# Two graph-attention networks on one core: heads turned through a direct SBUF exchange, two jobs of VectorE given to ScalarE, mask work and turns in other places

## The chip, the cores and the metric

The kernel runs on one core of one Trainium2 chip. The metric is device time in microseconds (us) of a whole launch; the kernel before takes 2327.34 us, the median of 3 runs (2326.52 to 2328.55).

## What is computed

Sixteen graphs of 512 nodes with 256 features pass through two networks. All is float32.

```python
# first network, 3 layers (L0)
si = x @ attn_w[l, :d];  sj = x @ attn_w[l, d:]
scores = leaky_relu(si[:, :, None] + sj[:, None, :] + attn_b[l])        # slope 0.2
attn = softmax(where(adjacency + I > 0, scores, -inf))
h = layernorm(x + attn @ x, g1[l], beta1[l])
x = layernorm(h + gelu(h @ W1[l] + b1[l]) @ W2[l] + b2[l], g2[l], beta2[l])
# x = layernorm(input + x), then the second network, 8 heads of 32 (L1)
xh = heads(x @ W_proj);  a_src, a_dst = xh . W_att
att = softmax(where(A > 0, leaky_relu(a_src + a_dst + b_att), -1e30))
out = relu(att @ xh)
# result: layernorm(x + out)
```

## The kernel before

Nodes lie on the 128 partitions in four groups (T = 4). A unit is one layer of one graph: 48 units, and the loop `for g in range(REGULAR)` takes them in a fixed order. A **slot** g runs, on TensorE (PE), the feed-forward of unit g and the attention of unit g+1; beside them the heads of the second network are made for older graphs. From slot 8 on the slots come in threes, and g % 3 says what else is in them. I call them kinds 2, 0 and 1, in the order in which they follow each other. Per graph, heads 0, 1, 2 are made in kind 2, heads 3, 4 in kind 0, heads 5, 6, 7 in kind 1. `turned(g)` are the heads made in the slot before; they have to change rows with columns before PE can use them. Two ways are used:

- heads 0, 3 and 5 are turned by PE (`turn`, PSUM bank pT) and copied back by ScalarE (ACT) (`turned_out`);
- heads 1, 2, 4, 6 and 7 (`moved`) are turned in 32x32 blocks by VectorE (DVE), L903 in `turn_blocks`, and the blocks then change partitions by DMA from SyncE's queue (SP), `move`, L410: four transfers out to `blocks_dram` (L416), a wait for all four, one transfer back (L419). 66 heads go this way.

PE uses four heads at once (`attend_heads`, L1282) in kinds 2 (heads 0 to 3) and 0 (heads 4 to 7), `heads_back` (L1290) follows two products later. In kind 2 that is after the first-layer product f = 1, in kind 0 after f = 3 (`spent_behind`).

PE's order in a slot: eight products f = 0 to 7 of the first feed-forward matrix (L1330), among them the spreading of a row of targets over the partitions (`first_target_row`, L1219, "trow"); then 16 **pieces** of the second matrix (L1341), and among these pieces the turns and products of the first network's attention (`attention`, L1240 and L1258), then the transposes of the new state (L1317). Three counts set how many pieces stand ahead of, inside and behind the attention. Product f = 0 waits until DVE has emptied bank 0 of the slot before (`fed_forward(graph, 0)`, L959), product f = 3 until it has emptied bank 1.

DVE's order in a slot is long and serial: end of the layer of the slot before (L959, L778, L966, L972), scores (L837), the masked targets and their maxima (L846, L853), the first network's exponents (L867 adds the maximum), the next head's targets, turns, the four groups of the attention (L913, L915, L920) with a head between them, the sums of an ended graph, mask work (`find_lone`, `make_masks`, `keep_masks`), the last head. ACT does leaky relu (L529, L536), exponentials (L542 for heads, L547 for the first network, out of pT), gelu (L560), normalisation (L576) and copies. POOL raises the variance to the power -1/2 (L500) and makes the shift (L505).

Every engine keeps its own order, written out by hand, and waits on semaphores. The functions that the change touches:

## Time and profile before

| | |
|---|---|
| median of 3 runs | 2327.34 us |
| profiled execution, its own time | 2329.5 us |
| its span | 2327.7 us |
| PE busy | 2187.7 us (94%) |
| DVE busy | 1863.9 us (80%) |
| ACT busy | 1636.4 us (70%) |
| DMA queue of SP | 313.72 MB, 42.5% of 16 engines |
| chain that ended last | PE 71%, DVE 20%, ACT 5% |
| mean granted PE clock | 0.984 |

The span is the time between the first and the last instruction that the profiler recorded. Busy time is the sum of the instructions of an engine; matmuls are pipelined, so PE's busy share is not its share of peak. A row of a timeline is start, duration, engine, line, operation, tiles, count and, in brackets, the idle time before it and what ended it. Consecutive instructions overlap a little in the records, so the step from one start to the next is what an instruction costs.

### The profile page before, as it was taken

The numbers are of one execution on the slowest core, as the hardware profiler recorded it, in microseconds if no ns is written. First come the engines' busy times: TensorE is split into PE (matmuls) and PEld (weight loads), VectorE is DVE, ScalarE is ACT, GpSimd is POOL, SyncE is SP. The second block draws the span as 40 slices with busy tenths as digits, with TensorE's granted clock in tenths as the row PEclk, the third lists the DMA queues.
The fourth block names the chain that finished last, engine by engine and source line by source line (L and its number), as shares of the span: only waits on it lengthen the run. The fifth ranks groups of instructions, "written<-read, shape, count | busy, mean of one in ns | idle before, by whom it ended". The sixth has DMA issues, their size and how long they took to land.

```text
span 2327.7 us, 31621 instructions
## 1 busy us (share of the span) xinstructions
PE 2187.7 (94%) x10117; PEld 1525.1 (66%) x10117; DVE 1863.9 (80%) x5743; ACT 1636.4 (70%) x3151; POOL 201.8 (9%) x200
## 2 busy tenths in 40 slices
PE   5999998999999999999999999999999999999766
PEld 3766666676667667667766766676676667667453
DVE  5566587688888888888888888888888888877867
ACT  2344467777787777778777777777777777778676
POOL 0000100010101001010100101010010101001000
PEclk9999999999999999999999999999999999999888
DMA  6011133227455362735436274553627455364201
GB/s 219 1 36 55 47 108 127 86 87 236 131 179 157 114 213 86 245 122 186 150 123 206 85 241 125 178 158 114 212 86 229 138 171 165 97 202 153 92 28 37
DMA packets 162145, 315.74 MB, mean 136 GB/s; under 512 B 10392, under 2 KB 82620, under 8 KB 153532
## 3 DMA queue, kind: packets, MB, share of 16 engines
q1 hardware_dynamic: 161980, 313.72, 42.5%
q8 instruction: 82, 1.34, 0.2%
q14 instruction: 83, 0.68, 0.1%
HBM read 235.82 MB, written 77.86 MB: 135 GB/s over the span
## 4 chain that ended last, share of the span: by engine, by line
PE 71%; DVE 20%; ACT 5%; issue 2%; POOL 1%; DMA 1%; DVEq 0%; SPq 0%; POOLq 0%; ACTq 0%
PE ffn L1341 19%; PE av L1258 14%; PE av L1330 10%; PE ffn L1330 10%; PE pT L1240 7%; PE av L1282 4%; DVE prob L846 3%; DVE prob L837 2%; DVE stats L778 2%; PE av L1317 1%; DVE lone L806 1%; PE av L1365 1%; PE trow L1365 1%; DVE xs L972 1%; DVE xs L966 1%
## 5 line engine op out<-in xcount | busy, mean ns | idle before, releaser
L1341 PE MATMUL ffn<-w_sb,G 128*128 128x256 f32 x3072 | 724.1, 381 | 12.5 <-ACT G L560 12.5
L1341 PEld LDWEIGHTS ffn<-w_sb,G 128*128 128x128 f32 x3072 | 571.1, 191 | 94.1 <-ACT G L560 18.1
L846 DVE CUSTOM_DVE_ANT_0 prob<-trow,mask 128x512 f32<-128x512 f32 x676 | 438.5, 686 | 31.7 <-PE trow L1219 19.6
L1330 PE MATMUL ffn<-hT,w_sb 128*128 128x512 f32 x768 | 364.0, 601 | 4.4 <-DVE xs L959 1.3
L1330 PE MATMUL av<-hT,w_sb 128*128 128x512 f32 x768 | 358.2, 596 | 0.0
L500 POOL TENSOR_TENSOR rstd<-veps,mhalf 128x4 f32<-128x4 f32 x127 | 170.5, 1342 | 2087.4 <-DVE veps L774 2087.4
L536 ACT ACTIVATE prob<-prob,s 128x512 f32<-128x512 f32 x484 | 329.4, 715 | 7.7 <-DVE aw_row L853 4.3
L542 ACT ACTIVATE prob<-prob,nm 128x512 f32<-128x512 f32 x464 | 329.2, 714 | 0.0
L1240 PEld LDWEIGHTS pT<-ident,prob 128*128 128x128 f32 x1648 | 208.2, 144 | 134.0 <-issue 103.3
L1240 PE MATMUL pT<-ident,prob 128*128 128x128 f32 x1648 | 251.3, 278 | 27.2 <-DVE prob L908 14.6
L1330 PEld LDWEIGHTS ffn<-hT,w_sb 128*128 128x128 f32 x768 | 140.1, 191 | 152.2 <-issue 134.1
L1330 PEld LDWEIGHTS av<-hT,w_sb 128*128 128x128 f32 x768 | 139.0, 191 | 148.3 <-issue 148.3
L560 ACT ACTIVATE G<-av,cols 128x512 f32<-128x512 f32 x192 | 130.1, 685 | 148.2 <-PE av L1330 148.1
L1258 PE MATMUL av<-xs,prob 128*128 128x257 f32 x960 | 229.9, 381 | 0.3 <-ACT prob L547 0.3
L560 ACT ACTIVATE G<-ffn,cols 128x512 f32<-128x512 f32 x192 | 131.4, 684 | 87.1 <-PE ffn L1330 86.6
L1258 PEld LDWEIGHTS av<-xs,prob 128*128 128x128 f32 x960 | 175.7, 190 | 22.5 <-ACT prob L547 0.7
L576 ACT ACTIVATE xs<-prob,shift,rstd 128x256 f32<-128x256 f32 x180 | 93.4, 590 | 133.3 <-POOL shift L505 133.2
L529 ACT ACTIVATE prob<-prob,small 128x512 f32<-128x512 f32 x192 | 128.6, 723 | 73.0 <-DVE small L853 73.0
L903 DVE STREAM_TRANSPOSE blocks<-prob 128x2048 f32<-128x2048 f32 x66 | 152.4, 2309 | 16.4 <-DMA blocks_dram<-blocks 16.0
L867 DVE TENSOR_SCALAR prob<-prob,small 128x512 f32<-128x512 f32 x192 | 93.3, 486 | 83.7 <-ACT prob L529 72.7
L547 ACT ACTIVATE prob<-pT 128x512 f32<-128x512 f32 x192 | 113.3, 591 | 54.0 <-PE pT L1240 53.5
L913 DVE RECIPROCAL small<-av 128x1 f32<-128x1 f32 x192 | 31.2, 163 | 137.5 <-PE av L1258 136.0
(164 smaller groups left out, 2739.5 us busy)
## 6 DMA issues: line engine op xcount, KB each, us to landing
w_sb<-in_L_gnn_W SPq DMA_DIRECT2D x92, 1024.0 KB, 8.8
blocks_dram<-blocks SPq DMA_DIRECT2D x264, 256.0 KB, 4.2
prob<-blocks_dram SPq DMA_DIRECT2D x66, 1024.0 KB, 4.9
trow<-rows_dram SPq DMA_DIRECT2D x127, 256.0 KB, 3.7
adj_sb<-in_adj SPq DMA_DIRECT2D x16, 1024.0 KB, 9.0
xin<-in_x SPq DMA_DIRECT2D x16, 512.0 KB, 6.0
x0r<-in_x SPq DMA_DIRECT2D x16, 512.0 KB, 10.0
out<-o SPq DMA_DIRECT2D x15, 512.0 KB, 6.9
```

The source lines that it names most:

```text
L500: nc.gpsimd.tensor_tensor(rstd[which][:], veps[which][:], mhalf[:], ALU.pow).then_inc(s_rstd, 1)
L529: nc.scalar.activation(prob0[:, t, :], prob0[:, t, :], ACT.Prelu, bias=col0[:, t:t + 1], scale=1.0, alpha=SLOPE).then_inc(s_score0, 1)
L536: nc.scalar.activation(m, m, ACT.Prelu, bias=s1[q // HEADS % 2][:, t, q % HEADS:q % HEADS + 1], scale=1.0, alpha=SLOPE).then_inc(s_score1, 1)
L542: nc.scalar.activation(m, m, ACT.Exp, bias=largest(q)[:, t:t + 1], scale=1.0, accum_out=sums_of(q)[:, 0, t:t + 1]).then_inc(s_exp, 1)
L547: nc.scalar.activation(prob0[:, t, :], pT[t % BANKS][:], ACT.Exp).then_inc(s_prob, 1)
L560: nc.scalar.activation(G[:, f, :], ff1[f % len(ff1)][:], ACT.Gelu, bias=b1_col[:, l, f:f + 1]).then_inc(s_gelu, 1)
L846: return v.tensor_tensor_reduce(out=out_[:, t, :], in0=targets, in1=mask[:, t, :], scale=1.0, scalar=LEAST, op0=ALU.add, op1=ALU.max, accu ...
L903: v.transpose(blocks[:].rearrange("p b (x i) -> p x b i", i=BLOCK), ring(q)[:].rearrange("p t (j b i) -> p (t j) b i", b=BLOCKS, i=BLOCK)) ...
L1240: last = te.transpose(pT[bank][:, j * P:(j + 1) * P], src[:, t, j * P:(j + 1) * P], ident[:])
L1258: last = te.matmul(av0[t % BANKS][:, 0:D + 1], prob0[:, t, j * P:(j + 1) * P], state(graph, l)[:, j, :], start=j == 0, stop=j == T - 1)
L1330: last = te.matmul(ff1[f % len(ff1)][:], w1_sb[:, weights_of(g) % STAGES, dt, f * P:(f + 1) * P], hT[:, dt, :], start=dt == 0, stop=dt == ...
L1341: last = te.matmul(ffn[part][:, at:at + D], G[:, f, t * P:(t + 1) * P], w2_sb[:, weights_of(g) % STAGES, f, :], start=f == 0, stop=f == FT ...
```

## The change

Line numbers of the kernel before are used throughout.

- `move` no longer goes through DRAM. For each turned head it issues 16 transfers from SBUF to SBUF, 32 partitions by 512 numbers (64 KB) each, all counted on one semaphore. DVE's next turn and PE's `attend_heads` wait for all 16.
- The first network's exponent leaves DVE: L867 is gone, ACT takes the maximum as the bias of its exponential in place (192 more instructions), and PE's turned result is copied out by ACT instead of going through the exponential. The interleaving of these with the exponentials of a held head ends: they come first, the held head's behind them.
- The normalisation of an ended graph (`graph_out`, L1047) moves to ACT in the regular slots.
- Turns are placed elsewhere: kind 0 now turns heads 1 (ahead of the attention) and 2 (behind it), kind 1 head 4 (ahead), kind 2 heads 6 and 7 as before. Before, kind 1 turned 2 and 4.
- `make_masks` is cut in two: `mask_edges` stands ahead of the attention of kind 0, `mask_diagonal` where it was, and `find_lone` moves to the end of kind 2.
- `spent_behind` is 1 in every slot (the change's condition on head 5 is false), so kind 0 attends heads 4 to 7 after f = 1 and takes them back after f = 3.
- The counts of pieces: one more ahead of the attention, one fewer behind it.

```diff
 def turned_ahead(g):
-    return [q for q in turned(g) if moved(q)][:1] if g % 3 != 1 else []
+    return [q for q in turned(g) if moved(q)][:1] if g > min(FIRST_MADE) + 1 else []
 def turned_behind(g):
-    if g % 3 == 1:
-        return [q for q in turned(g - 1) + turned(g) if moved(q)][-2:] if g > 1 else []
-    return [q for q in turned(g) if moved(q)][1:] if g % 3 == 2 else []
+    return [q for q in turned(g) if moved(q)][len(turned_ahead(g)):]
 def spent_behind(g):
-    return 3 if g % 3 == 0 else 1
+    return 4 if g % 3 == 0 and HEADS - 3 in BY_BLOCKS else 1
+def masked(g):
+    return g // 3 + 1 if g > 3 and g % 3 == 0 and g // 3 + 1 < GRAPHS else None
...
             def move(q):
                 n = moves(q) - 1
-                i = n % BANKS
                 sp.wait_ge(s_block, n + 1)
-                if n >= BANKS:
-                    sp.wait_ge(s_moved, 16 * (n - BANKS + 1))
-                for a in range(BLOCKS):
-                    sp.dma_start(blocks_dram[i, :, :, a, :].rearrange("b j n -> j b n"),
-                                 blocks[a * BLOCK:(a + 1) * BLOCK, :, :]).then_inc(s_left, 16)
-                sp.wait_ge(s_left, 16 * BLOCKS * (n + 1))
-                sp.dma_start(ring(q)[:], blocks_dram[i].rearrange("b j a n -> (b j) a n")).then_inc(s_moved, 16)
+                for b in range(BLOCKS):
+                    for a in range(BLOCKS):
+                        sp.dma_start(ring(q)[b * BLOCK:(b + 1) * BLOCK, a, :],
+                                     blocks[a * BLOCK:(a + 1) * BLOCK, b, :]).then_inc(s_moved, 16)
...
+            def first_exponential(t):
+                act.wait_ge(s_score0, c("score0"))
+                nc.scalar.activation(prob0[:, t, :], prob0[:, t, :], ACT.Exp, bias=nm0[:, t:t + 1], scale=1.0).then_inc(s_arg, 1)
             def probabilities(t):
                 act.wait_ge(s_pt, c("pt"))
-                nc.scalar.activation(prob0[:, t, :], pT[t % BANKS][:], ACT.Exp).then_inc(s_prob, 1)
+                nc.scalar.copy(prob0[:, t, :], pT[t % BANKS][:]).then_inc(s_prob, 1)
+            def first_network_probabilities(u, scored):
+                first_exponential(0)
+                for t in range(1, T):
+                    if t >= scored:
+                        score0(u, t)
+                    first_exponential(t)
+                    probabilities(t - 1)
+                probabilities(T - 1)
...
+                if leaving(g) is not None:
+                    normalise(LAST, o1, o1, s_out)
...
                 for q in turned_ahead(g):
                     turn_blocks(q)
+                if masked(g) is not None:
+                    mask_edges(masked(g) % 2)
                 attention(graph2, l2, *new[1:2])
...
                 elif g > 3 and g % 3 == 2:
                     keep_masks(g // 3 % 2)
-                elif g > 3 and g % 3 == 0 and g // 3 + 1 < GRAPHS:
-                    find_lone((g // 3 + 1) % 2)
-                    make_masks((g // 3 + 1) % 2)
+                    if g // 3 + 2 < GRAPHS:
+                        find_lone(g // 3 % 2)
+                elif masked(g) is not None:
+                    mask_diagonal(masked(g) % 2)
...
-                ahead, inside, behind = (4, (1, 1), (1, 1, 1, 1)) if four is None else (2, (2, 1), (2, 1, 2, 1))
+                ahead, inside, behind = (5, (1, 1), (1, 1, 1, 0)) if four is None else (3, (2, 1), (2, 1, 1, 1))
```

Three places show the order before and now. First DVE at the end of a slot of kind 2, from the turn of head 7 (`prob_7`) to the emptying of bank 1 (second L959; in the change L974) and the statistics behind it. Before:

```order
L903 STREAM_TRANSPOSE blocks<-prob_7 128x16x4x32
L951 TENSOR_TENSOR xs<-xs,bias_row 128x4x256
L959 TENSOR_TENSOR xs<-ffn,xs 128x2x256
L816 COPY mask_0<-mask_0 128x2048
L819 SCALAR_TENSOR_TENSOR mask_0<-ident,own,mask_0 128x128 x4
L824 TENSOR_SCALAR mask_0<-mask_0,lone 128x512 x4
L846 ISA prob_2,small<-trow,mask_1 128x512
```

In the change:

```order
L918 STREAM_TRANSPOSE blocks<-prob_7 128x16x4x32
L966 TENSOR_TENSOR xs<-xs,bias_row 128x4x256
L974 TENSOR_TENSOR xs<-ffn,xs 128x2x256
L835 COPY mask_0<-mask_0 128x2048
L838 SCALAR_TENSOR_TENSOR mask_0<-ident,own,mask_0 128x128 x4
L843 TENSOR_SCALAR mask_0<-mask_0,lone 128x512 x4
L825 TENSOR_REDUCE lone<-adj_sb 128x4
L827 TENSOR_SCALAR lone<-lone 128x4
L829 TENSOR_SCALAR lone<-lone 128x4
L865 ISA prob_2,small<-trow,mask_1 128x512
```

Three instructions of `find_lone` are new here, ahead of head 2 (`prob_2`). Second, DVE in a slot of kind 0, from the maxima of head 4 to the emptying of bank 0. Before:

```order
L853 SCALAR_TENSOR_TENSOR nm<-small 128x4
L1039 SCALAR_TENSOR_TENSOR o<-o,l1x 128x1024
L778 BN_STATS stats<-o 128x6 x4
L769 BN_AGGR mv_out<-stats 128x2 x4
L774 TENSOR_SCALAR veps<-mv_out 128x4
L951 TENSOR_TENSOR xs<-xs,bias_row 128x4x256
L959 TENSOR_TENSOR xs<-ffn,xs 128x2x256
L806 TENSOR_REDUCE lone<-adj_sb 128x4
```

In the change:

```order
L872 SCALAR_TENSOR_TENSOR nm<-small 128x4
L918 STREAM_TRANSPOSE blocks<-prob_2 128x16x4x32
L1054 SCALAR_TENSOR_TENSOR o<-o,l1x 128x1024
L796 BN_STATS stats<-o 128x6 x4
L787 BN_AGGR mv_out<-stats 128x2 x4
L791 TENSOR_SCALAR mv_out<-mv_out 128x4
L792 TENSOR_SCALAR veps<-mv_out 128x4
L966 TENSOR_TENSOR xs<-xs,bias_row 128x4x256
L974 TENSOR_TENSOR xs<-ffn,xs 128x2x256
L815 TENSOR_SCALAR mask_0<-mask_0 128x128
```

The turn of head 2 now stands between the attention and the emptying of bank 0; the first mask instructions behind it are gone. Third, ACT in a slot of kind 2 behind the gelus, down to the normalisation. Before (`prob` is the first network's tile, `prob_2` or `prob_7` the held head, the other one the new head):

```order
L547 ACTIVATE prob<-pT 128x512
L542 ACTIVATE prob_7,sums<-prob_7,nm 128x512
L536 ACTIVATE prob_0<-prob_0,s_0 128x512
L542 ACTIVATE prob_0,sums<-prob_0,nm 128x512 x4
L576 ACTIVATE xs<-prob,shift,rstd 128x256 x4
```

with the first three rows standing four times. In the change:

```order
L550 ACTIVATE prob<-prob,small 128x512 x2
L554 COPY prob<-pT 128x512
L532 ACTIVATE prob<-prob,small 128x512
L550 ACTIVATE prob<-prob,small 128x512
L554 COPY prob<-pT 128x512
L532 ACTIVATE prob<-prob,small 128x512
L550 ACTIVATE prob<-prob,small 128x512
L554 COPY prob<-pT 128x512 x2
L545 ACTIVATE prob_7,sums<-prob_7,nm 128x512
L539 ACTIVATE prob_0<-prob_0,s_0 128x512
```

The held head's four exponentials now begin only behind the last copy of the first network, and four exponentials are new.

## Rows read from the trace of the kernel before

**Rows 1.** The page, engines: busy us (share of the span) and instructions.

```profile
PE 2187.7 (94%) x10117; PEld 1525.1 (66%) x10117; DVE 1863.9 (80%) x5743; ACT 1636.4 (70%) x3151; POOL 201.8 (9%) x200
```

**Rows 2.** Waits of PE, 220 to 2060 us: total us, times, longest.

```profile
PE ffn L1341 <- ACT G L560: 12.5, 14, 0.9
PE av L1258 <- issue: 10.5, 14, 0.8
PE av L1282 <- issue: 9.2, 10, 1.8
```

**Rows 3.** Timeline of PE, end of a kind 2 slot and kind 0's products.

```profile
1107.77 7.07 PE L1341 MATMUL ffn<-w_sb,G 128*128 128x256 f32 x32
1114.67 1.04 PE L1317 MATMUL av<-ident,xs 128*128 128x128 f32 x8
...
1118.14 1.88 PE L1330 MATMUL ffn<-hT,w_sb 128*128 128x512 f32 x4
1119.86 3.60 PE L1330 MATMUL av<-hT,w_sb 128*128 128x512 f32 x8
...
1130.49 0.60 PE L1240 MATMUL pT<-ident,prob 128*128 128x128 f32 x4
1131.08 0.65 PE L1219 MATMUL trow<-ident,raw 128*128 128x128 f32 x4
```

**Rows 4.** Timeline of DVE over the same stretch.

```profile
1107.97 0.17 DVE L913 RECIPROCAL small<-av 128x1 f32<-128x1 f32 x1 [0.97 <-PE av L1258]
...
1111.65 2.31 DVE L903 STREAM_TRANSPOSE blocks<-prob 128x2048 f32<-128x2048 f32 x1
1130.94 0.08 DVE L837 DVE_READ_ACCUMULATOR2_ANT raw<- 128x1 f32 x1
```

**Rows 5.** Timeline of DVE, end of the kind 0 slot that follows.

```profile
1151.72 0.17 DVE L913 RECIPROCAL small<-av 128x1 f32<-128x1 f32 x1 [0.97 <-PE av L1258]
...
1160.23 0.69 DVE L959 TENSOR_TENSOR xs<-ffn,xs 128x512 f32<-128x512 f32 x1
1160.84 2.27 DVE L806 TENSOR_REDUCE lone<-adj_sb 128x4 f32<-128x2048 int32 x1
...
1163.55 1.23 DVE L789 TENSOR_SCALAR mask<-adj_sb 128x2048 bf16<-128x2048 int32 x1
```

**Rows 6.** Timeline of PE, end of that kind 0 slot.

```profile
1158.84 1.09 PE L1317 MATMUL av<-ident,xs 128*128 128x128 f32 x8 [0.24 <-ACT xs L576]
...
1162.36 1.88 PE L1330 MATMUL ffn<-hT,w_sb 128*128 128x512 f32 x4
```

**Rows 7.** Timeline of ACT in the kind 2 slot, before and at the normalisation.

```profile
1104.20 0.71 ACT L542 ACTIVATE prob<-prob,nm 128x512 f32<-128x512 f32 x1
...
1104.90 0.71 ACT L536 ACTIVATE prob<-prob,s 128x512 f32<-128x512 f32 x1
1105.51 0.71 ACT L542 ACTIVATE prob<-prob,nm 128x512 f32<-128x512 f32 x1
...
1111.88 2.08 ACT L576 ACTIVATE xs<-prob,shift,rstd 128x256 f32<-128x256 f32 x4 [3.45 <-POOL shift L505]
```

**Rows 8.** The page, groups of instructions: count | busy us, mean ns | idle before, releaser.

```profile
L867 DVE TENSOR_SCALAR prob<-prob,small 128x512 f32<-128x512 f32 x192 | 93.3, 486 | 83.7 <-ACT prob L529 72.7
```

**Rows 9.** DMA issues on the page: count, KB each, us from issue to landing.

```profile
blocks_dram<-blocks SPq DMA_DIRECT2D x264, 256.0 KB, 4.2
prob<-blocks_dram SPq DMA_DIRECT2D x66, 1024.0 KB, 4.9
```

**Rows 10.** The view of DMA issues: the last graph's two stores.

```profile
out<-o SPq DMA_DIRECT2D x2, 256.0 KB, 2.1
```

**Rows 11.** Timeline of SP's queue: issuing one head out and back, kind 2.

```profile
1113.99 2.71 SPq L416 DMA_DIRECT2D blocks_dram<-blocks  x4
...
1119.92 0.34 SPq L419 DMA_DIRECT2D prob<-blocks_dram  x1
```

**Rows 12.** Timeline of PE, the transposes of one of the first slots.

```profile
79.59 1.09 PE L1317 MATMUL av<-ident,xs 128*128 128x128 f32 x8 [1.44 <-ACT xs L576]
```

More of the change, by code:

```diff
@@ L232, in build @@
         nmean, shift = ([sb(f"{name}{i}", [P, T]) for i in range(2)] for name in ("nmean", "shift"))
+        nmean.append(mv_out[:, :, 0])
+        shift.append(mv_out[:, :, 1])
         first_xs = prob1[6][:].rearrange("p t n -> p (t n)")[:, 0:T * (D + 1)].rearrange("p (t d) -> p t d", t=T)
@@ L289, in build @@
         s_av1, s_oT, s_back, s_av1e = sem("av1"), sem("oT"), sem("back"), sem("av1e")
-        s_ve, s_rstd, s_shift = sem("ve"), sem("rstd"), [sem("shift0"), sem("shift1")]
+        s_ve, s_rstd, s_shift = sem("ve"), sem("rstd"), [sem(f"shift{i}") for i in range(3)]
         s_hn, s_hT, s_hTe, s_ff1, s_gelu = sem("hn"), sem("hT"), sem("hTe"), sem("ff1"), sem("gelu")
@@ L601, in _ @@
                 score0(0, t)
-            for t in range(T):
-                probabilities(t)
+            first_network_probabilities(0, T)
             act.wait_ge(s_colT, 1)
@@ L678, in _ @@
                 gelu(1, f)
-                if f >= T:
+                if f >= T and not moved(first - 2):
                     turned_out(first - 2, f - T)
@@ L702, in _ @@
                 score0(UNITS - 2, t)
-            for t in range(T):
-                probabilities(t)
+            first_network_probabilities(UNITS - 2, T)
             for t in range(T):
@@ L1046, in graph_out @@
                 for t in range(T):
-                    last = v.tensor_scalar(o1[:, t, :], o1[:, t, :], mv_out[:, t, 0:1], rstd[LAST][:, t:t + 1],
-                                           ALU.subtract, ALU.mult)
+                    last = v.tensor_scalar(o1[:, t, :], o1[:, t, :], nmean[LAST][:, t:t + 1], rstd[LAST][:, t:t + 1],
+                                           ALU.add, ALU.mult)
                 last.then_inc(s_out, 1)
@@ L1067, in _ @@
             find_lone(0)
-            make_masks(0)
+            mask_edges(0)
+            mask_diagonal(0)
             dve.wait_ge(s_aw, 32)
@@ L1071, in _ @@
             first_targets(0)
-            for t in range(T):
-                first_exponents(t)
             dve.wait_ge(s_const, 16 * CONSTS)
@@ L1079, in _ @@
             find_lone(1)
-            make_masks(1)
+            mask_edges(1)
+            mask_diagonal(1)
             for g in range(REGULAR):
@@ L1147, in _ @@
             plus_bias(GRAPHS - 1, 1)
-            turn_blocks(first - 3)
+            for q in turned_ahead(REGULAR):
+                turn_blocks(q)
             head_made(second)
             fed_forward(GRAPHS - 1, 0)
-            turn_blocks(first - 1)
+            for q in turned_behind(REGULAR):
+                turn_blocks(q)
             head_made(third)
@@ L1160, in _ @@
             first_targets(1)
-            for t in range(T):
-                first_exponents(t)
             graph_begins(GRAPHS - 2)
@@ L1268, in attend_heads @@
             def attend_heads(q):
-                by_act, by_vector = all_out[[h for h in range(q, q + SIDE) if not moved(h)][-1], T - 1]
-                pe.wait_ge(s_prob, by_act)
-                if by_vector:
-                    pe.wait_ge(s_copy, by_vector)
+                by_engine = [h for h in range(q, q + SIDE) if not moved(h)]
+                if by_engine:
+                    by_act, by_vector = all_out[by_engine[-1], T - 1]
+                    pe.wait_ge(s_prob, by_act)
+                    if by_vector:
+                        pe.wait_ge(s_copy, by_vector)
                 if any(moved(q + i) for i in range(SIDE)):
-                    pe.wait_ge(s_moved, 16 * moves(q + SIDE - 1))
+                    pe.wait_ge(s_moved, 16 * BLOCKS * BLOCKS * moves(q + SIDE - 1))
                 pe.wait_ge(s_x1Te, turning[0])
@@ L1417, in _ @@
                         for q in heads[:1]:
-                            turn(q, f - T)
+                            if not moved(q):
+                                turn(q, f - T)
                 pieces(ahead)
@@ L1446, in _ @@
                 first_product(REGULAR, f)
-                if f >= T:
+                if f >= T and not moved(first - 2):
                     turn(first - 2, f - T)
```

45 lines of the change are left out of this document (20 added, 25 removed).

## The prediction

> **What bounds the kernel now.** I began with the engines' busy shares: PE 94%, DVE 80%, ACT 70% [rows 1]. PE is the bound, and what DVE and ACT save or gain matters only where PE waits for them. So the second view was the waits of PE over the regular slots: twelve to fourteen times some 0.9 us for the last gelu, as often 0.75 us for the first network's probabilities just behind it, both in kind 1, and ten times before the four heads of kind 2, 9.2 us in all [rows 2]. They come to under 33 us, and that is nearly all that a perfect rearrangement could win there. The third view was the timelines of PE and DVE side by side. I measure in them from A, the start of DVE's reciprocal after the last product of the attention: there DVE has waited 0.97 us for PE [rows 4, 5], so up to A it is PE that sets the pace. Behind A DVE runs without a pause of more than 0.2 us until the raw scores of the next slot, and PE's trow waits for these: the turn before it has begun at 1130.49 and takes a step of 0.44, trow begins at 1131.08, 0.15 late [rows 3, 4]. DVE has no slack at all in this place, though it idles 20% of the span.
>
> **Kind 2 into kind 0.** Before, trow begins 23.11 us after A. Of that 23.05 are DVE's work, and PE alone would be there after 22.96. The change puts `find_lone` into DVE's part. Its cost is the step from its start to that of the next mask instruction, 1160.84 to 1163.55, 2.71 us [rows 5]. DVE gives up nothing between A and the raw scores, so trow begins at A + 25.8. PE is there at 22.96, less 0.86 for the piece moved ahead of A, plus 0.44 for `heads_back`, which now precedes trow, plus about 0.4 for a wait at the transposes (next paragraph): 22.9. It waits 2.9 us instead of 0.15. The stretch costs 0.86 ahead of A, plus 2.71, less the 0.44 that comes out of the stretch behind trow: **+3.1 us**.
>
> **The transposes of kind 2.** The extra work of ACT is four exponentials in place, 0.61 each going by the step of the prelu over the same shape (1104.90 to 1105.51) [rows 7]. They fit in ahead of the attention. What moves is the held head: its exponentials (step 0.70, 1104.20 to 1104.90) and the new head's prelus and exponentials now start behind the last copy, some 3.8 us before A by PE's steps (the attend product 1.74, a piece 0.86, another product 1.74, less a copy of 0.5). 4 x 0.70 + 4 x 0.61 + 4 x 0.70 = 8.0 us, so ACT is free at A + 4.2. The shift is there at A + 3.9 (1111.88). The normalisation of 2.08 ends at A + 6.3, and PE with seven pieces arrives at A + 5.84 instead of 6.70 [rows 3, 7]. The wait is 0.4 to 0.5. It could be nothing, or 1.5 if the interleaving hid more than I see.
>
> **Kind 0 into kind 1.** Bank 0 is emptied from 1160.23, done at the next start, 1160.84: A + 9.12 [rows 5]. The turn of head 2 now stands before it, 2.31 us [rows 4], with a small `nmean` of under 0.1. That makes A + 11.5. PE, whose f = 0 began at 1162.36, A + 10.64 with a wait of 0.24 [rows 6], would be there at about 9.8, a piece earlier. It waits 1.7 us. With the piece ahead of A the slot costs 0.86 + 11.5 - 10.64 = **+1.7 us**. `mask_edges` costs nothing: it stands ahead of the attention in the place of the exponents that DVE gives up (4 x 0.49) [rows 8], and if PE were there first it would cost up to 2.2. The mask work behind bank 0 shrinks by `find_lone`'s 2.7 and the 1.23 and more of the edges [rows 5] against 2.3 of the turn, so the maxima that kind 1 waits for come at least 1.6 us earlier relative to A, while PE comes 0.9 later.
>
> **Kind 1.** That takes away the 0.91 and 0.79 of [rows 2] and two slips of 0.1 and 0.2 before trow: **-2.1 us**. Against it stands the state of a begun graph: behind the last copy ACT has 4 x 0.61, a normalisation of 2.0, 4 x 0.70 and two copies, 8.2 us, and PE, now with no piece between the second transposition and the projection, waits for the second copy: about **+1.0 us**, between 0.5 (the copy alone) and 2.
>
> **The wait at the heads of kind 2** goes with head 2 moved a slot earlier: 9.2 us in all [rows 2].
>
> **The exchange.** Issuing went by 0.68 a transfer for the four out and 0.34 for the one in [rows 11], landing took 4.2 and 4.9 [rows 9], and the shortest landing of a quarter megabyte was 2.1 [rows 10]. No row shows 64 KB between two places in SBUF. The access is as plain as the one in, so I take 0.34: 16 x 0.34 + 2.1 = 7.5 us from the end of the turn; the upper bound is 16 x 0.68 + 4.2 = 15.1. Before, it was from the turn's end at 1113.96 to 1119.92 + 4.9, 10.9 us [rows 4, 9, 11]. Kind 0's heads are now due after two products, 3.4 us behind f = 0: A + 13.1 (two steps of 1.72, 1118.14 to 1119.86 [rows 3]), and the turn of head 7 ends at A + 6.0. The 7.1 us there are met within 0.4, and 2.9 more are free, since PE waits for trow just behind. The halved DRAM traffic is worth nothing here, because nothing on PE's path waits for bandwidth.
>
> **The sum.** Twelve rounds of three slots have the mask work. 12 x (3.1 + 1.7 - 2.1 + 1.0) = 44, less 9 for the heads of kind 2. In five early slots PE already waits about 1.4 us for the normalisation [rows 12], and one piece less behind A adds 0.86 each: 4. At the first attention and the last, PE waits for ACT, whose chain grows by one exponential before the turn and some more behind it: 2 each (0 to 4). The two slots with four heads, where ACT is full, another 2 (-3 to 6). 44 - 9 + 4 + 4 + 2 = 45 us. On the profiled execution's own 2329.5 (span 2327.7) that is about 2375; the median of the runs is 2 us lower, so I say **2372 us**, with 2348 to 2396 for this case: the bounds of the terms add up to about 24 either way.
>
> **Rivals.**
> - **PE stays the only bound.** The waits of [rows 2] go, the two DVE waits and ACT's do not come. Then 12 x 2.1 and 9.2 are won, 34 us: 2293, or 2300 with the starts and ends. For it speaks that DVE loses 4 x 0.49 a slot and ACT has 30% to spare. Against it: none of DVE's savings lies between A and the places where PE waits. It decides if DVE reaches A with PE behind it by over 3 us.
> - **The exchange is slow at issue.** With 0.68 and 4.2, kind 0's heads come 8.0 us late, 5.1 more than is free; 13 times, +66: 2438.
> - **The transfers go one after another.** 16 x 2.1 = 34 us a head, 24 more than is free, 13 times: near 2680. Against it: the four transfers out were issued within 2.71 us and landed in 4.2 each, so they overlap [rows 9, 11]. The Trainium skill, "DMA: Bandwidth & Descriptors" (Anatomy of one DMA), gives every transfer a fixed cost of about 2 us and puts half efficiency at 860 KB, which speaks against cutting a megabyte into pieces of 64 KB; its fit would make one such transfer 2.15 us as an estimate, and sixteen in a row 34. The trace of before agrees with the fixed part as a latency, not as time in which nothing else moves.
> - **The change evens out.** DVE's waits come but are hidden behind each other or behind ACT's: 2320 to 2335.
>
> **Chances.** My case 0.58, PE alone 0.20, slow issue 0.11, one after another 0.03, evened out 0.08. The range 2298 to 2405 takes in my case, the evened one and most of the fast one, and leaves out the slow exchanges and the fastest corner. No change means within 0.2%, about what a measurement of this kernel can tell: the evened case gives 0.05 of it and 0.03 of faster. Faster 0.23, same 0.05, slower 0.72.
>
> **What would show it.** In the profile of the changed kernel: PE at trow waiting some 3 us for DVE's raw in every kind 0 slot; PE at f = 0 of kind 1 waiting 1.5 us for DVE's L974; waits at the projection of kind 1 of about 1 us on ACT's copies; no gelu wait in kind 1; no wait at the heads of kind 2; DVE busy down by the 93 us of L867 [rows 8] and the graphs' normalisation, ACT up by over 100; 1056 transfers of 64 KB at 0.34 each. I am wrong if PE reaches trow later than raw, or if the transfers take their 0.68.

## The result, and the profile after

The changed kernel takes **2447.47 us** (median of 4 runs, 2445.24 to 2450.13) against 2327.95 in the same session: a ratio of 1.0515, 95% interval 1.0497 to 1.0533. It is slower, as forecast, but by 120 us and not by 45, and outside the range. The profiled execution's span is 2443.5 us against 2327.7, 115.8 more, and the later tables account for these. From one use of the heads of kind 2 to the next, over eleven rounds of three slots, the changed kernel takes 144.07 us and the kernel before 135.98 (554.77 to 2139.56 and 537.14 to 2032.92). That is 8.1 a round, 97 for twelve rounds; the other 19 lie in the first slots and the last. The forecast had 2.9 a round and 10 outside.

The engines on the page, to be put beside [rows 1]:

```profile
PE 2219.7 (91%) x10117; PEld 1528.7 (63%) x10117; DVE 1760.4 (72%) x5514; ACT 1793.9 (73%) x3395; POOL 204.1 (8%) x213
```

DVE has lost 103 us of work and ACT has gained 157, as the change says. PE executes the same 10117 instructions, but is busy 32.0 us longer and idle 83.8 us longer (223.8 against 140.0). So there are two costs, one in waiting and one in the products themselves. The groups of PE by line, busy time and mean on the left of the last bar, idle time just before them and its releaser on the right, first of the kernel before:

```profile
L1330 PE MATMUL ffn<-hT,w_sb 128*128 128x512 f32 x768 | 364.0, 601 | 4.4 <-DVE xs L959 1.3 <-issue 0.9 <-ACT hT L555 0.9
...
L1240 PE MATMUL pT<-ident,prob 128*128 128x128 f32 x1648 | 251.3, 278 | 27.2 <-DVE prob L908 14.6 <-DVE prob L867 6.4 <-ACT prob L551 5.8
...
L1258 PE MATMUL av<-xin,prob 128*128 128x257 f32 x512 | 124.6, 386 | 10.5 <-issue 10.5
L1282 PE MATMUL av<-prob,xp 128*32 128x512 f32 x960 | 114.1, 598 | 9.5 <-issue 9.2
L1317 PE MATMUL av<-ident,xs 128*128 128x128 f32 x360 | 49.4, 282 | 12.6 <-ACT xs L576 12.6
...
L1219 PE MATMUL trow<-ident,raw 128*128 128x128 f32 x196 | 31.7, 286 | 25.0 <-DVE raw L837 24.0
```

and of the change (L1346, L1254, L1272, L1298, L1333, L1381 and L1233 are L1330, L1240, L1258, L1282, L1317, L1365 and L1219 of before; L1272 has no idle time left before it):

```profile
L1357 PE MATMUL ffn<-w_sb,G 128*128 128x256 f32 x3072 | 723.2, 381 | 5.5 <-ACT G L577 5.5
...
L1346 PE MATMUL ffn<-hT,w_sb 128*128 128x512 f32 x768 | 362.5, 599 | 21.5 <-DVE xs L974 16.9 <-ACT G L577 2.6 <-ACT hT L572 1.1
L1254 PE MATMUL pT<-ident,prob 128*128 128x128 f32 x1648 | 253.1, 279 | 50.9 <-ACT prob L550 27.2 <-DVE prob L923 14.8 <-ACT prob L568 8.5
...
L1298 PE MATMUL av<-prob,xp 128*32 128x512 f32 x960 | 137.0, 702 | 51.0 <-issue 51.0
L1333 PE MATMUL av<-ident,xs 128*128 128x128 f32 x360 | 49.4, 281 | 21.0 <-ACT xs L593 21.0
L1381 PE MATMUL av<-wp_sb,xin 128*128 128x272 f32 x128 | 36.0, 404 | 13.3 <-ACT xin L605 13.3
...
L1233 PE MATMUL trow<-ident,raw 128*128 128x128 f32 x196 | 30.5, 279 | 19.4 <-DVE raw L856 19.4
```

Idle time, after less before: the attending heads +41.5, the transposes `pT` +23.7, the first product, most of it at f = 0, +17.1, the projection +13.3 (from nothing), the state transposes +8.4; back come 10.5 at the probabilities of kind 1, 7.0 at the gelus (5.5 where [rows 2] have 12.5) and 5.6 at trow. That makes 80.9 of the 83.8. Of the 32 us of busy time, 22.9 lie in the attending heads: the same 960 products take 702 ns in place of 598.

The place where both fall together is kind 0. PE, with the idle time in brackets:

```profile
1181.13 5.09 PE L1298 MATMUL av<-prob,xp 128*32 128x512 f32 x32 [4.24 <-issue]
1186.15 1.98 PE L1346 MATMUL av<-hT,w_sb 128*128 128x512 f32 x4
...
1192.28 0.60 PE L1233 MATMUL trow<-ident,raw 128*128 128x128 f32 x4
```

SP's queue before and during it, and the DMA issues on the page (KB each, us to landing):

```profile
1169.44 10.00 SPq L421 DMA_DIRECT2D prob<-blocks  x16
```

```profile
prob<-blocks SPq DMA_DIRECT2D x1056, 64.0 KB, 2.0
```

Sixteen transfers take SP 10.0 us to issue, 0.63 each, and the last lands 2.0 later, at about 1181.4 by these numbers; the products begin at 1181.13. And the clock, in windows over the same stretch (us, PE's busy time and count, granted clock, DMA share, GB/s):

```profile
1173.29:1176.80 3.51, 3.51 (x9) 1.00 0.41 102
1176.80:1181.10 4.30, 0.09 (x1) 0.95 0.40 105
1181.10:1186.15 5.05, 5.02 (x32) 0.70 0.77 263
1186.15:1191.00 4.85, 4.85 (x19) 1.00 0.59 205
```

The products behind the pause run at a mean granted clock of 0.70, part of the stretch at the lower of the two levels, and take 5.05 us; in the kernel before the same 32 products have a step of 3.57 (1078.11 to 1081.68). Trow then waits for nothing: DVE's raw scores, which I had forecast to be 2.9 us late, are there.

### The profile page after: what moved, and what is told of

Its sections match the earlier page's. It is cut to its first block, busy times and chain, and to the rows that moved or that the text cites. A ratio compares the mean times of both kernels' runs of the same rounds, so it can differ in the third digit from the quotient of the medians.

```text
span 2443.5 us, 32337 instructions
## 1 busy us (share of the span) xinstructions
PE 2219.7 (91%) x10117; PEld 1528.7 (63%) x10117; DVE 1760.4 (72%) x5514; ACT 1793.9 (73%) x3395; POOL 204.1 (8%) x213
## 4 chain that ended last, share of the span: by engine, by line
PE 60%; ACT 26%; DVE 9%; issue 3%; POOL 1%; DMA 0%; DVEq 0%; POOLq 0%; ACTq 0%
PE av L1346 14%; PE ffn L1346 11%; PE ffn L1357 10%; PE av L1272 8%; ACT prob L545 8%; PE pT L1254 7%; PE av L1298 5%; ACT prob L539 5%; ACT prob L532 2%; ACT L550 2%; DVE prob L865 2%; ACT G L577 2%; PE av L1333 2%; ACT xs L593 1%; ACT prob L568 1%
## 5 line engine op out<-in xcount | busy, mean ns | idle before, releaser
L865 DVE CUSTOM_DVE_ANT_0 prob<-trow,mask 128x512 f32<-128x512 f32 x676 | 432.9, 686 | 82.7 <-PE trow L1233 70.7
L1346 PE MATMUL ffn<-hT,w_sb 128*128 128x512 f32 x768 | 362.5, 599 | 21.5 <-DVE xs L974 16.9
L1346 PE MATMUL av<-hT,w_sb 128*128 128x512 f32 x768 | 363.9, 601 | 0.0
L1254 PEld LDWEIGHTS pT<-ident,prob 128*128 128x128 f32 x1648 | 204.9, 144 | 176.9 <-issue 113.8
L1254 PE MATMUL pT<-ident,prob 128*128 128x128 f32 x1648 | 253.1, 279 | 50.9 <-ACT prob L550 27.2
L1346 PEld LDWEIGHTS ffn<-hT,w_sb 128*128 128x128 f32 x768 | 140.2, 191 | 157.8 <-issue 150.6
L1346 PEld LDWEIGHTS av<-hT,w_sb 128*128 128x128 f32 x768 | 138.7, 193 | 154.8 <-issue 154.8
L1272 PE MATMUL av<-xs,prob 128*128 128x257 f32 x960 | 230.2, 382 | 0.0
L1272 PEld LDWEIGHTS av<-xs,prob 128*128 128x128 f32 x960 | 176.3, 191 | 22.2 <-ACT prob L554 0.2
L1298 PE MATMUL av<-prob,xp 128*32 128x512 f32 x960 | 137.0, 702 | 51.0 <-issue 51.0
L554 ACT COPY prob<-pT 128x512 f32<-128x512 f32 x192 | 111.6, 581 | 97.1 <-PE pT L1254 91.8
L532 ACT ACTIVATE prob<-prob,small 128x512 f32<-128x512 f32 x192 | 133.3, 722 | 62.0 <-DVE small L872 62.0
L550 ACT ACTIVATE prob<-prob,small 128x512 f32<-128x512 f32 x192 | 133.4, 718 | 3.6
```

The costliest lines, as they stand in the source:

```text
L532: nc.scalar.activation(prob0[:, t, :], prob0[:, t, :], ACT.Prelu, bias=col0[:, t:t + 1], scale=1.0, alpha=SLOPE).then_inc(s_score0, 1)
L550: nc.scalar.activation(prob0[:, t, :], prob0[:, t, :], ACT.Exp, bias=nm0[:, t:t + 1], scale=1.0).then_inc(s_arg, 1)
L865: return v.tensor_tensor_reduce(out=out_[:, t, :], in0=targets, in1=mask[:, t, :], scale=1.0, scalar=LEAST, op0=ALU.add, op1=ALU.max, accu ...
L1254: last = te.transpose(pT[bank][:, j * P:(j + 1) * P], src[:, t, j * P:(j + 1) * P], ident[:])
L1272: last = te.matmul(av0[t % BANKS][:, 0:D + 1], prob0[:, t, j * P:(j + 1) * P], state(graph, l)[:, j, :], start=j == 0, stop=j == T - 1)
L1298: last = te.matmul(av1[i * HD:(i + 1) * HD, :], xp[q // HEADS % 2][:, j, q % HEADS + i, :], sources(q + i, j), start=j == 0, stop=j == T - 1)
```

## The experiments

Twelve kernels in three sessions; ratios are to the kernel before in the same session. Differences between two changed kernels are taken from their medians as they stand; the kernel before moved between 2327.95 and 2330.40 from one session to another, so such a difference can be off by up to 2.5 us.

### Where the cost of the exchange is: three kernels

**e1**: the change, with the attending heads of kind 0 two products later, behind f = 3 as in the kernel before.

```
-    return 4 if g % 3 == 0 and HEADS - 3 in BY_BLOCKS else 1
+    return 3 if g % 3 == 0 else 1
```

> The change, but kind 0 attends its four heads behind product f = 3 again, as before. Theory A (the issue of 16 transfers, 0.63 us each, makes head 7 late; PE waits 4.2 us and runs the heads' products at a lower granted clock behind that wait): the wait falls to about 0.8, the products take 3.64 again instead of about 5.1, and the wait for DVE's raw scores at trow, 2.5 us, that the forecast named comes into sight: about 2.4 us less a round of three slots, 2418 us. Rival B (that wait at trow is not there): 4.9 us less a round, 2389. Rival C (the heads have nothing to do with it): 2447.

Measured 2411.74 us, ratio 1.0356 (1.0338 to 1.0373): 35.7 less than the change. The heads wait 0.8 us in all and are back at 608 ns. But the whole round did not come back. Waits of PE between 600 and 2100 us (total, times, longest), of the change and then of e1:

```profile
PE av L1298 <- issue: 46.7, 11, 4.5
PE ffn L1346 <- DVE xs L974: 14.3, 11, 1.3
```

```profile
PE ffn L1346 <- DVE xs L974: 38.2, 22, 2.4
...
PE trow L1233 <- DVE raw L856: 3.7, 6, 0.6
```

Once PE is earlier, the product at f = 3, which needs bank 1 emptied by DVE, waits 2.1 (2.4 twice), and in six of the eleven rounds trow waits 0.6 behind it. Together that is 2.7 where I had forecast 2.9 for `find_lone`, though most of it one step ahead of trow. In the change it was hidden behind the late heads. In the other five rounds, every second one, the same wait at f = 3 is followed by a slower product, and trow then finds its row ready:

```profile
1026.85 3.44 PE L1346 MATMUL ffn<-hT,w_sb 128*128 128x512 f32 x4 [2.12 <-DVE xs L974]
1168.83 1.98 PE L1346 MATMUL ffn<-hT,w_sb 128*128 128x512 f32 x4 [2.12 <-DVE xs L974]
```

The mean granted clock was 0.56 in the first of these products and 1.00 in the second. Between the profiled spans (2443.5 and 2409.6) lie 33.9 us: 11.4 of PE's busy time (2219.7 against 2208.3) and 22.5 of its idle time, which is the heads' wait gone less what grew at DVE's emptied banks.

**e2**: the change, with the way through DRAM of the kernel before.

```
-                for b in range(BLOCKS):
-                    for a in range(BLOCKS):
-                        sp.dma_start(ring(q)[...], blocks[...]).then_inc(s_moved, 16)
+                for a in range(BLOCKS):
+                    sp.dma_start(blocks_dram[i, :, :, a, :]..., blocks[...]).then_inc(s_left, 16)
+                sp.wait_ge(s_left, 16 * BLOCKS * (n + 1))
+                sp.dma_start(ring(q)[:], blocks_dram[i]...).then_inc(s_moved, 16)
```

> The change, but with the exchange through DRAM of the kernel before. Theory A: from the end of a turn to the landing it took 10.9 us before and takes 10.0 + 2.0 now, so heads 4 to 7 arrive 1.2 us earlier and PE waits 3.0 instead of 4.2: 2432 us. Rival C (the direct transfers cost by something else than being late, contention in SBUF for instance): most of the 119 us goes, 2330 to 2380.

Measured 2434.86, ratio 1.0452 (1.0436 to 1.0467). The heads still wait 3.5 us, 3.8 at most, and a product still takes 683 ns in the mean:

```profile
PE av L1302 <- issue: 38.7, 11, 3.8
```

So the path by itself is 12.6 us of the loss in this order, and the place in PE's order more: neither way of exchanging makes the earlier place. **e4** asks the same of the kernel before: its DRAM path replaced by the sixteen direct transfers, nothing else.

> The kernel before with the direct exchange alone. Theory A: heads 4 to 7 land at A + 18.1 and PE is there at A + 17.1, about 1 us of wait a round; DVE's turn of head 4, 6 us behind that of head 2, waits for its landing, some 6 us, and pushes the raw scores of kind 2 behind PE's trow by 2 to 3: 3.5 us a round, 2373 us. Rival C (the transfers cost by being there): over 2400. Rival D (the direct exchange is no worse than the one through DRAM): 2327 within 5.

Measured 2376.8, ratio 1.02 (1.0185 to 1.0216), as expected to within 4 us. The waits between 600 and 2100 us:

```profile
PE trow L1215 <- DVE raw L833: 16.5, 11, 1.8
PE av L1278 <- issue: 14.8, 15, 1.2
```

The heads that wait here are mainly those of kind 0, some 1.1 us a round (1141.27, for one); those of kind 2 wait 3.8 us in five places, where the kernel before has 9.0 in nine. The larger part of the 47 us comes by another way: over the whole kernel PE's waits rise by 7.6 us at the heads, but by 24.8 at trow and 11.0 at the emptied banks, and the trace shows why. Through DRAM, DVE may fill `blocks` again once the four transfers out have landed; with the direct exchange only once all sixteen have. Waits of DVE's turns from 220 to 2060 us, of the kernel before and then of e4:

```profile
DVE blocks L903 <- DMA blocks_dram<-blocks: 7.9, 7, 1.6
DVE blocks L899 <- DMA prob<-blocks: 79.7, 21, 6.8
```

In the round at 1090 the turn waits 5.62 for the landing, and PE's trow then waits 1.28 for the raw scores (1101.60). In the change the turns stand further apart, and none of them waits for a landing: this is the difference that the traces show between the 47 us here and the 12.6 there.

### DVE's part

**e3**: e1, with `find_lone` back in kind 0, ahead of `mask_diagonal`.

```
                     keep_masks(g // 3 % 2)
-                    if g // 3 + 2 < GRAPHS:
-                        find_lone(g // 3 % 2)
                 elif masked(g) is not None:
+                    find_lone(masked(g) % 2)
                     mask_diagonal(masked(g) % 2)
```

> As e1_heads_f3, and find_lone goes back from the end of kind 2 to the end of kind 0, ahead of mask_diagonal. Theory A: no wait at trow of kind 0 any more (2.5 us a round less than e1_heads_f3), but DVE's maxima for kind 1 come 2.7 later and bring back about 1 us of the gelu wait there: 2400 us against 2418 of e1_heads_f3. Rival B (no wait at trow, so nothing to be won): as e1_heads_f3 or 10 us slower.

Measured 2386.29, ratio 1.0243 (1.0228 to 1.0259): 25.4 us less than e1, 2.1 a round for 12 rounds, of the 2.71 that DVE needs for it. The gelus of kind 1 wait again, as in the kernel before (9.7 us in eleven places), because DVE is later there. The heads of kind 0 wait too: PE no longer waits at f = 3, comes to them earlier, and finds the exchange of 12.0 us not quite done even behind f = 3:

```profile
PE ffn L1345 <- DVE xs L974: 15.4, 11, 1.6
...
PE av L1297 <- issue: 9.8, 11, 1.2
```

The first line is the emptying of bank 0 behind the turn of head 2, 1.4 a slot where the forecast said 1.7.

### ACT's part

**e5**: the kernel before, with ACT's exponentials in place and DVE's additions gone, the held head's exponentials behind them instead of between them, and with the change's counts of pieces.

```
-            def first_exponents(t):
-                v.tensor_scalar(prob0[:, t, :], prob0[:, t, :], nm0[:, t:t + 1], None, ALU.add)...
+            def first_exponential(t):
+                nc.scalar.activation(prob0[:, t, :], prob0[:, t, :], ACT.Exp, bias=nm0[:, t:t + 1], ...)...
...
-                nc.scalar.activation(prob0[:, t, :], pT[t % BANKS][:], ACT.Exp).then_inc(s_prob, 1)
+                nc.scalar.copy(prob0[:, t, :], pT[t % BANKS][:]).then_inc(s_prob, 1)
...
-ahead, inside, behind = (4, (1, 1), (1, 1, 1, 1)) if four is None else (2, (2, 1), (2, 1, 2, 1))
+ahead, inside, behind = (5, (1, 1), (1, 1, 1, 0)) if four is None else (3, (2, 1), (2, 1, 1, 1))
```

> The kernel before with one part of the change alone: ACT takes the first network's exponentials and copies pT out, and one piece moves from behind the attention to ahead of it. Theory A, by the waits that the change's profile shows: 0.4 us at each turn of kinds 2 and 0, 0.35 at the transposes of kind 2, about 1.1 there in kind 0 (the shift of POOL is slow again behind the graph's sum), 0.5 and 1.05 in kind 1, 0.86 in each of the five first slots: about 3 us a round more, 2372 us. Rival E (ACT has room, the part is free): 2325 to 2335.

Measured 2389.02, ratio 1.0251 (1.0236 to 1.0267): 59 us, and 17 more than expected. This kernel has neither the direct exchange nor the moved turns and mask work, so it is ACT's part alone, with its counts. A round takes 139.36 us, 3.4 more than before (41 for twelve), and some 18 lie outside the rounds. The waits between 600 and 2100 us:

```profile
PE av L1317 <- ACT xs L589: 16.0, 21, 1.4
PE pT L1240 <- ACT prob L547: 13.8, 32, 0.5
PE av L1365 <- ACT xin L601: 11.6, 11, 1.1
```

The middle line was in no part of my forecast. It comes once in nearly every slot, 32 times in 33 slots, of every kind. ACT around it, before:

```profile
1095.64 1.36 ACT L529 ACTIVATE prob<-prob,small 128x512 f32<-128x512 f32 x2
1097.02 1.28 ACT L547 ACT_TABLE_LOAD   x1
1098.31 0.60 ACT L547 ACTIVATE prob<-pT 128x512 f32<-128x512 f32 x1
```

and in the changed kernel, with PE's transpose below it:

```profile
1149.18 0.59 ACT L568 COPY prob<-pT 128x512 f32<-128x512 f32 x1
1149.79 1.28 ACT L550 ACT_TABLE_LOAD   x1
1151.08 1.33 ACT L550 ACTIVATE prob<-prob,small 128x512 f32<-128x512 f32 x2
1152.55 0.59 ACT L554 COPY prob<-pT 128x512 f32<-128x512 f32 x1
```

```profile
1148.71 2.76 PE L1357 MATMUL ffn<-w_sb,G 128*128 128x256 f32 x12
1151.86 0.66 PE L1254 MATMUL pT<-ident,prob 128*128 128x128 f32 x4 [0.39 <-ACT prob L550]
```

Before, PE transposed what DVE had added, and only then ACT took the exponential on the way out of PSUM: the load of its table, 1.28 us, ran while PE transposed and went on with its pieces (1096.44 to 1098.61). Now the first exponential is wanted ahead of the transposition, so gelu, copy, table load and exponential stand in a row in front of PE. The change's piece ahead of the transposes covers 0.86 of that and leaves 0.4 to 0.5. No run takes the table load or the end of the interleaving away by itself, so their shares of the 59 us are read from the timeline and not measured.

**e6** takes that cover away: e5 with the old counts of pieces (the last pair of lines of its diff undone).

> The kernel before with ScalarE's exponentials of the first network, but with the old counts for the pieces of the layer behind (two of four and three of four, in place of three and two). The same with the new counts took 2389 us against 2330: transposes of kind 1 and 2 wait 0.5 for their exponential (31 times), state transposes 1.4 in kind 2 and the projection 1.1. Theory A: ScalarE's own queue is what costs, and the counts only choose who waits: the transposes' wait goes from 0.5 up to about 1.3, the projection's and the state transposes' get smaller, and the time is 2385 to 2400. Theory B: moving a piece ahead of an exponential is itself the cost, and the old counts give back most of it: below 2375.

Measured 2393.39, ratio 1.028 (1.0263 to 1.0297), as theory A said:

```profile
PE pT L1240 <- ACT prob L547: 41.5, 32, 1.4
...
PE av L1317 <- ACT xs L589: 2.9, 11, 0.5
PE av L1365 <- ACT xin L601: 2.1, 11, 0.2
```

The 32 waits grow from 0.43 to 1.30, by a piece, and most of those at the state transposes and the projection go. The change's new counts are right, and worth 4 to 6 us; what costs is ACT's chain, which PE meets in one place or the other.

### Can the direct exchange be had more cheaply?

**e7**: e4, with eight of the sixteen transfers issued by SP and eight by GpSimd's queue, on a semaphore of its own.

> The kernel before with the direct exchange, eight of the sixteen transfers issued by SP and eight by GpSimd's queue. Theory A: what made the direct exchange slow is the issuing, one after another on one queue; halved, a head lands 5.0 + 2.0 = 7 us behind its turn instead of 12.1, less than the 10.9 through DRAM. No wait at the heads, none of DVE for the blocks: 2318 to 2325 us. Rival C (the transfers themselves are slow): 2360 or more. A GpSimd issue of over 1.2 us each would also bring the loss back, and is seen on its queue.

Measured 2364.14, ratio 1.0145 (1.013 to 1.016): the expectation was missed by 40 us. The issues did halve, but they stand in GpSimd's order ahead of work that DVE waits for. GpSimd in kind 1:

```profile
1091.47 3.91 POOL L499 DMA_DIRECT2D prob<-blocks  x8 [9.45 <-DVE blocks L918]
1095.40 1.03 POOL L504 TENSOR_TENSOR rstd<-veps,mhalf 128x4 f32<-128x4 f32 x1
```

**c2** puts these behind the next slot's deviations.

```
+                for q in late:
+                    move(q)
...
-                for q in turned_behind(g)[1:]:
-                    move(q)
+                late = turned_behind(g)[1:]
```

> The kernel before with the direct exchange, eight transfers by SP and eight by GpSimd's queue, as in the run of 2364 us, but GpSimd issues those of heads 5 to 7 behind the next slot's deviations, so that these no longer stand behind 4 us of issues. Theory A: in the run of 2364 VectorE waited for GpSimd's deviation behind the issues and PE for VectorE (3.9 us, 8 times, and more in early slots); with the order changed this goes, and the exchange is still no later than 5.7 + 2.5 = 8.2 us: 2325 to 2340. Theory B: the many small transfers cost something else (their landing, or SBUF ports) that the order does not touch: 2355 to 2370.

Measured 2337.7, ratio 1.0038 (1.0023 to 1.0053): 26 us back, within theory A's 2325 to 2340, with the deviation first (1090.40) and the issues behind it (1091.57). The small transfers are then 9 us dearer than the way through DRAM, not cheaper: four waits of up to 2.8 are left at the heads of kind 2 in the earlier rounds, and SP and GpSimd together issue sixteen transfers a head where there were five.

**e8**: the kernel before through DRAM, two of the four transfers out by GpSimd's queue; **c3**: the same behind the deviations.

> The kernel before, through DRAM, two of the four transfers out issued by GpSimd's queue. Theory A: 1.35 us of issue less on the way of a head, so the waits of 1.1 to 1.8 us at the heads of kind 2 in the later rounds go: 2320 us. If these waits are of something else: 2327.

> The kernel before with its exchange through DRAM, two of the four transfers out by GpSimd's queue, these issued behind the next slot's deviations. With the issues ahead of the deviations it took 2347, the heads' products waiting 3.3 us in 14 places since GpSimd's second transfer came late. Theory A: what cost was the place in GpSimd's order: 2320 to 2335. Theory B: GpSimd's landing of 5.1 us against SP's 3.7 is what is late, so nothing changes: 2340 to 2350.

Measured 2347.46, ratio 1.0072 (1.0057 to 1.0087), and 2338.52, ratio 1.0037 (1.0023 to 1.0052). Neither wins. c3 came out between its two theories: the place in GpSimd's order was worth 9 us. The other 10 fit the longer landing on GpSimd's queue, which no run took away; here on the page of c3:

```profile
blocks_dram<-blocks SPq DMA_DIRECT2D x132, 256.0 KB, 3.7
blocks_dram<-blocks POOLq DMA_DIRECT2D x132, 256.0 KB, 5.1
```

**c4**: the kernel before, out in one transfer of 128 partitions, back in four.

```
-                for a in range(BLOCKS):
-                    sp.dma_start(blocks_dram[i, :, :, a, :]..., blocks[a * BLOCK:(a + 1) * BLOCK, :, :])...
+                sp.dma_start(blocks_dram[i], blocks[:]).then_inc(s_left, 16)
...
-                sp.dma_start(ring(q)[:], blocks_dram[i]...)...
+                for b in range(BLOCKS):
+                    sp.dma_start(ring(q)[b * BLOCK:(b + 1) * BLOCK, :, :], blocks_dram[i, :, b, :]...)...
```

> The kernel before with its exchange through DRAM, but the way out is one transfer of all 128 partitions in place of four of 32; the four on the way in stay. Theory A: each issue costs SP 0.6 us or more where the transfer touches 32 partitions, so one issue in place of four ends the exchange about 1.5 us earlier, and the waits of the attending heads of 1.1 to 1.8 us shrink: 2320 to 2327. Theory B: the landing of one large transfer takes as much longer as the issues are fewer (the longest of four ends it either way): 2328 to 2335.

Measured 2333.38 over 10 runs, ratio 1.0023 (1.0013 to 1.0032): theory B, a hair slower. SP for head 7:

```profile
1116.68 0.34 SPq L415 DMA_DIRECT2D blocks_dram<-blocks  x1
1122.41 1.74 SPq L418 DMA_DIRECT2D prob<-blocks_dram  x4
```

The issue out fell from 2.71 to 0.34 [rows 11], yet the way back starts 5.73 behind it where it was 5.93, since the one large transfer took 5.7 to land (4.8 is the median) where none of the four took more than 4.4; and the four issues of the way back then cost 1.4 more.

### The change, mended

**c1**: the change with most of what the runs had shown to cost moved (`find_lone` stays at the end of kind 2): exchange through DRAM, heads of kind 0 behind f = 3, `keep_masks` ahead of kind 2's attention, `mask_diagonal` ahead of the ended graph's sum, bank 0 emptied ahead of the turn of head 2, the copies of a begun state one exponential earlier.

```
+                if g > 3 and g % 3 == 2:
+                    keep_masks(g // 3 % 2)
                 attention(graph2, l2, *new[1:2])
-                for q in turned_behind(g)[:1]:
+                for q in turned_behind(g)[:1] if g % 3 else []:
                     turn_blocks(q)
+                if masked(g) is not None:
+                    mask_diagonal(masked(g) % 2)
...
                 fed_forward(graph, 0)
+                for q in turned_behind(g)[:1] if g % 3 == 0 else []:
+                    turn_blocks(q)
```

> The change with what the runs point to: exchange through DRAM, heads of kind 0 behind f = 3, keep_masks ahead of the attention of kind 2, mask_diagonal ahead of the graph's sum and head 2's turn behind the emptying of bank 0, the two copies of a begun graph's state ahead of the last two exponentials. Theory A: of the 7 us of waits a round in e3_f3_lone go 1.05 at the heads, 0.8 at bank 0, 0.7 at the gelu and 0.8 at the projection: 2386 - 12 x 3.3 = 2346 us. Rival (other waits take their place): 2375 to 2390.

Measured 2354.56, ratio 1.0104 (1.0087 to 1.0121), 9 above theory A's 2346. Of the 120 us, 93 are back. Most of what PE still waits for is ACT: of 40.2 us between 600 and 2060 us, 32.5 end on ACT, and 7.5 on the emptying of bank 0 by DVE. The largest is the line of e5 again:

```profile
PE pT L1264 <- ACT prob L554: 13.8, 32, 0.5
```

ACT's whole part is in this kernel, 59 us in e5, and it is yet only 24 above the kernel before. The waits at kind 1's probabilities and kind 2's heads (10.5 and 9.0) are gone and 7.0 of the gelus' 12.5: the moves of work do win what the forecast had seen there.

No kernel of the twelve beats the one before.

## Why the forecast was wrong, point by point

**What bounds the kernel** held. DVE has 103 us less to do and the kernel is 120 slower: what was lost is 83.8 us in which PE waited and 32.0 in which its products took longer, 22.9 of these at the heads behind their wait.

**Two steps failed**, the price of the exchange and the price of ACT's exponentials, and either by itself is too small to explain the miss: with the heads on time (e1) the kernel still takes 2411.7, above the range's 2405.

**The exchange** is the first. I took 0.34 us an issue "as plain as the one in"; it is 0.63 (0.51 to 0.59 for the instruction, and the gap to the next), near the mean of 0.68 out to DRAM that I had kept as the upper end. With 10.0 for sixteen and 2.0 of landing it is 12.0 where I had 7.5, inside my two ends of 7.5 and 15.1 but on the wrong side of the 10.0 (7.1 and 2.9) that is free. PE waits 4.2 a slot. The rival of the slow issue names this mechanism and comes to 2438; it was the case that happened, though its landing of 4.2 was twice the measured 2.0 and its exchange of 15.1 us 3.1 too long. That 2438 lies so near to 2447 is in part luck: the rival gives the heads 66 us where the runs give 36, and has no more for ACT than my case. No row showed this form, the two ends lay on both sides of what decides, and I took the one that looked alike; with the price so open the slow case deserved far more than 0.11.

It then missed that **a pause is paid twice**: 4.24 of waiting and 1.48 (5.05 less 3.57) of slower products, some twelve times. e1 removes both at the heads, though slower products come back at f = 3 in every second round.

**Kind 2 into kind 0**, +3.1: right in size, wrong in what is seen. The change shows no wait at trow at all, which by my own text makes me wrong there; but e1 shows 2.1 + 0.6 as soon as the heads are on time, and e3 gets 25 us back by taking `find_lone` out. The cost was hidden under the larger one, as the text allowed ("2.9 more are free, since PE waits for trow just behind"). It doesn't add to the heads' 4.2: of the two, the longer counts.

**Kind 0 into kind 1**, 1.7: measured 1.3 in the change and 1.4 in e3. **The transposes of kind 2**, 0.4 to 0.5: 0.35 shown (1169.77, where ACT's normalisation ends). **The projection**, 1.0: 1.05. **The gains**: the 10.5 at kind 1's probabilities and the 9.2 at kind 2's heads came whole, of the gelus' 12.5 only 7.0.

**ACT's exponentials** are the second step that failed. They were priced at nothing beside the attention ("They fit in ahead of the attention"). That was wrong: in the change PE waits 27.2 us for them, about half of it 0.4 to 0.5 at a time in nearly every slot, where the table load came to stand ahead of the transposition, the rest in a few places at the start and the end (6.4 the longest). I had summed ACT's durations and not asked what the first one waits for. e5 shows the whole of ACT's part alone at 59 us, where my sum has 22 for it (12 at the projection, 10 for the starts, the ends and the slots with four heads).

**The sum**, roughly, by the runs: 36 for the heads with the exchange (the change to e1), 25 for `find_lone` (e1 to e3), 57 for the rest (e3 at 2386, and e5, ACT alone, at 2389: the moved turn of head 2 gains at kind 2's heads and loses at bank 0). Of the 75 us between forecast and measurement, the exchange makes 36, priced at nothing, and ACT's part 37 (59 less 22). The other terms missed in both directions, and that the parts simply add up is not shown.

**The sign** held, and for the reason given against the rival that PE stays the only bound: none of what DVE saves lies where PE waits for it behind A. It doesn't come from the missed exchange alone: c1, with the exchange undone and the order mended, is still 24 us slower.

**One after another** is excluded: sixteen transfers were done 12.0 us after the first issue, not 34. The Trainium skill, "DMA: Bandwidth & Descriptors" (Anatomy of one DMA), gives a fixed cost of about 2 us to a transfer issued by GpSimd. The 2.4 us from issue to landing on GpSimd's queue (e7) and the 2.0 on SP's are near it, as a latency that overlaps with the next issues. What the sixteen add up to is the issue on SP's queue, 0.63 each.

## What to carry to other kernels

A route that saves a trip through DRAM but cuts a transfer into pieces is paid in issue time on one queue: multiply the pieces by the issue and compare with the window in PE's order before the consumer, and where no row shows that form of transfer, reason from the dearest issue first. Ask too how long the transfers hold the buffer that they read: the next writer of it may wait where the consumer does not (e4). When an operation moves from one side of a transposition to the other, look at what its engine must do just before it (here a table load), for that comes onto the path even when the engine has time in all. And of two delays that end at the same place only the longer shows: take it away, and look again before you call the other one free.

## What the runs showed of the hardware

- Issue time on SP's queue goes with the form of the transfer, and varies within a form. SBUF to SBUF, 32 partitions and 64 KB: 0.51 the shortest, 0.59 the median, and with the gap 0.63 in the mean of sixteen (2.06 the longest of all). From 32 partitions to DRAM, 256 KB: of four in a row 0.32 the shortest, 0.51 the median and 1.24 the longest, but only 0.38 each when two are sent (e8). From DRAM to 32 partitions 0.43 (c4), and 0.34 for 128 partitions in either direction. The 0.68 of the four out [rows 11] was therefore no price of one, and the premise of c4 fell with it. GpSimd's queue issues the SBUF form in 0.50 and lands it in 2.4, but lands a quarter megabyte in DRAM in 5.1 against 3.7.
- After 4.24 us without a product, the next 5.05 us ran at a mean granted clock of 0.70, then at 1.00 again, and the heads' products were slower behind all twelve such waits. Behind shorter waits it goes either way, and not by the length of the wait: c2 has 5.34 us for the heads behind a wait of 2.04 (granted clock 0.67), e2 has 3.64 behind 3.41 (1.00), and in e1 the same 2.12 is followed by 0.56 and by 1.00. What decides, no run separates.

```profile
1085.44 5.34 PE L1300 MATMUL av<-prob,xp 128*32 128x512 f32 x32 [2.04 <-issue]
1605.46 3.64 PE L1302 MATMUL av<-prob,xp 128*32 128x512 f32 x32 [3.41 <-issue]
```

- A wait costs more than its row says. Matmuls overlap at their ends (four transposes are busy 0.60 at a step of 0.43), and a pause ends that: three pieces and the transposes' start took 3.15 (1148.71 to 1151.86) where the step without a wait is 2.59, so 0.56 for a wait shown as 0.39. In e5 a round is 3.4 us longer, of which the listed waits explain 2.3 (56.4 us against 30.7 between 600 and 2100 us, eleven rounds); five more waits a round at 0.17 each would be 0.85 of the missing 1.1, an estimate from these rows.
